# Layer norms of a transformer kernel: root on ScalarE and reciprocal on VectorE, or a power on GpSimd

## The chip, the cores and the metric

The kernel runs on one core of one Trainium2 chip. The metric is the device time of one execution in microseconds (us), and several executions are summed up by their median. TensorE (PE in the rows) multiplies matrices, VectorE (DVE) and ScalarE (ACT) do elementwise work and reductions, GpSimd (POOL) does elementwise work in on-chip memory only, and SyncE (SP) issues the transfers. Each engine works through its own queue in order, and they wait for each other on semaphores.

## What is computed

2048 tokens of width 128 pass through six residual blocks, each behind a layer norm. Stage A is a coupled feed-forward net, B a causal attention, C the feed-forward net again, D a mixture of eight experts, E an attention with low-rank updates, and F the mixture again. Block B also ends in a norm of its own with scale and offset, called M here. Only the norm matters for the change:

```python
def _layernorm(x, axis=-1, eps=1e-05):
    m = jnp.mean(x, axis=axis, keepdims=True)
    v = jnp.var(x, axis=axis, keepdims=True)
    return (x - m) / jnp.sqrt(v + eps)

x = L0_attn_target
x = x + 0.5 * _L0_ffn_ref(_layernorm(x, axis=-1), ...)   # A
x = x + _L0_attn_ref(_layernorm(x, axis=-1), ...)        # B; norm M inside
x = x + 0.5 * _L0_ffn_ref(_layernorm(x, axis=-1), ...)   # C
x = x + 0.5 * _L1_ffn_ref(_layernorm(x, axis=-1), ...)   # D
x = x + _L1_attn_ref(_layernorm(x, axis=-1), ...)        # E
x = x + 0.5 * _L1_ffn_ref(_layernorm(x, axis=-1), ...)   # F
```

## The kernel before, in words

The activations lie feature by feature on the 128 partitions, with the 2048 tokens along the free axis, cut into four chunks of 512 (`NC = 4`, `CW = 512`). The order of work on every engine is written out by hand, and nothing is scheduled by a planner around the norms. The norms are called `LN_A` to `LN_F` and `LN_M`.

A norm of one chunk is a relay over three engines, each step a method of class `Norm`:

1. `pe_centre` (line 274): TensorE multiplies by a centring matrix. The result is x minus its mean, in a PSUM bank.
2. `act_square` (line 325) squares it on ScalarE, and `dve_centre` (line 297) copies it to `m_cen` on VectorE.
3. `pe_var` (line 282): four small products sum the squares over the features. The variances of the 512 tokens lie in a 128x128 block.
4. `act_root` (line 336): ScalarE takes the root of variance plus epsilon, into `m_std`, 128x128 per chunk.
5. `dve_invert` (line 307): VectorE takes the reciprocal of `m_std` in place.
6. `pe_spread` (line 289): four products spread the reciprocals back over all partitions.
7. `dve_norm` (line 311) or `dve_affine` multiplies and gives the normed chunk.

TensorE, ScalarE and VectorE take their steps of the four chunks interleaved, so that one chunk's step on an engine stands in the queue between steps of other chunks. `LN_M` and `LN_C` go in pairs of chunks: LN_M 0 and 1, LN_M 2 and 3, LN_C 0 and 1, LN_C 2 and 3, and each pair's `pe_var` stands behind the `pe_spread` of the pair before it on TensorE. `LN_D` runs into stage D, and `LN_E` and `LN_F` are interleaved with the end of the stage before and the start of their own; chunk 0 of LN_E and chunk 3 of LN_F lie inside an expert stage.

ScalarE's functions come out of loaded tables. `warm(function)` (line 2000) is a tiny activation that is there to bring in a table early, as `warm(ACT.Sqrt)` ahead of the norms; where there is none, the load stands in front of the activation that needs it (lines 336, 829, 801). GpSimd has other work near the norms: `pool_low` (line 1263) makes the third bf16 part of queries and keys from each chunk of an attention, and the expert stage's `pool` (lines 790, 792) splits each normed chunk.

Of the kernel before, what the change touches and what calls it, by code (L numbers as in the profile page):

```python
# [9 lines left out]
fp32 = mybir.dt.float32  # L10
# [71 lines left out]
class Constants:  # L82
# [7 lines left out]
    def __init__(self, nc, n, dram, k):  # L90
# [12 lines left out]
        k["eps"] = n.sb("eps", [P, 1], fp32)  # L103
        k["fold"] = n.sb("fold", [P, 2], fp32)
# [82 lines left out]
    def dve(self, dve):  # L187
        nc, k = self.nc, self.k
        nc.vector.memset(k["eps"][:, :], EPS)
        for b, sign in enumerate((1.0, -1.0, -1.0, 1.0)):  # L190
            nc.vector.memset(k["sign"][32 * b:32 * b + 32, :], sign)
# [69 lines left out]
class Norm:  # L261


    def __init__(self, nc, n, ps, k, centres=True):
        self.nc, self.ps, self.k = nc, ps, k
# [20 lines left out]
    def pe_spread(self, pe, i, c, bank):  # L286
        pe.wait_ge(self.inverted, NC * i + c + 1)
        for u in range(TPC):
# [16 lines left out]
    def dve_invert(self, dve, i, c):  # L305
        dve.wait_ge(self.std_ready, NC * i + c + 1)
        self.nc.vector.reciprocal(self.std[:, c, :], self.std[:, c, :]).then_inc(self.inverted, 1)  # L307

# [25 lines left out]
    def act_root(self, act, i, c, bank):  # L334
        act.wait_ge(self.var_ready, NC * i + c + 1)
        self.nc.scalar.activation(self.std[:, c, :], self.ps[:, bank, 0:TW], ACT.Sqrt, bias=self.k["eps"][:, 0:1])\
# [288 lines left out]
class Experts:  # L625
# [157 lines left out]
    def pool(self, pool):  # L783
        k = self.k
        for c in range(NC):
            pool.wait_ge(self.norm.out, NC * self.ln + c + 1)
# [51 lines left out]
    def dve(self, dve):  # L838
# [99 lines left out]
        else:  # L938
# [11 lines left out]
            norm.dve_invert(dve, self.ln, last)  # L950
            add(1)
            norm.dve_norm(dve, self.ln, last, self.xn, self.SPARE)
        for i in range(self.begin, len(steps)):
# [16 lines left out]
            if ln is not None:  # L970
                if i == 11:
                    norm.dve_centre(dve, ln, 0, self.SPARE)
                elif i == 14:
                    norm.dve_invert(dve, ln, 0)
# [736 lines left out]
def macaron(nc, dram, out):  # L1711
    with ExitStack() as stack:
# [50 lines left out]
        with nc.Block() as block:  # L1763
# [14 lines left out]
            def _(pool):  # L1778
                constants.pool(pool)
                for c in range(NC):  # L1780
                    att_b.pool_low(pool, c)
                att_b.pool_loop(pool)
                constants.pool_experts(pool)
                moe_d.pool(pool)
                for c in range(NC):
                    att_e.pool_low(pool, c)
                att_e.pool_loop(pool)
                moe_f.pool(pool)
# [112 lines left out]
            def _(dve):  # L1901
# [15 lines left out]
                def ffn_end(ffn, ln, bank):  # L1917
# [5 lines left out]
                    norm.dve_invert(dve, ln, 0)  # L1923
                    norm.dve_centre(dve, ln, 3, bank + 3)
                    norm.dve_invert(dve, ln, 1)
                    norm.dve_norm(dve, ln, 0, xn, bank)
                    norm.dve_invert(dve, ln, 2)
                    norm.dve_norm(dve, ln, 1, xn, bank + 1)
                    norm.dve_invert(dve, ln, 3)
# [15 lines left out]
                def b_end(phase, c):  # L1945
# [7 lines left out]
                    elif phase == 2:  # L1953
                        norm_m.dve_invert(dve, LN_M, c)
                    elif phase == 3:
                        norm_m.dve_affine(dve, LN_M, c, xn, x, NC + c, x_done)
                    elif phase == 5:
                        norm.dve_invert(dve, LN_C, c)
# [18 lines left out]
                norm.dve_invert(dve, LN_E, 1)  # L1977
# [3 lines left out]
                norm.dve_invert(dve, LN_E, 2)  # L1981
                norm.dve_invert(dve, LN_E, 3)
# [5 lines left out]
                norm.dve_invert(dve, LN_F, 0)  # L1988
                norm.dve_invert(dve, LN_F, 1)
# [137 lines left out]
```

## Time and profile before

| | us |
|---|---|
| three runs | 1308.64, 1314.72, 1324.19 (median 1314.72) |
| the profiled execution | 1311.64 |
| its span from first to last instruction | 1309.8 |
| PE busy | 1246.0 (95%) |
| DVE busy | 1147.0 (88%) |
| ACT busy | 1061.3 (81%) |
| POOL busy | 183.0 (14%) |

The profiled execution's own time is 1.8 us more than its span. Busy shares are averages over stages with different limits: both attentions together fill the stretches from about 75 to 456 us and from about 616 to 1233 us, and the norms in question lie in the short stretches between.

### The profile page before, as it was taken

How to read it: one execution, taken by the hardware profiler on the slowest of the kernel's cores; microseconds unless marked ns; L12 is line 12 of the kernel's file. 1: busy time of each engine (PE TensorE's matmuls, PEld its weight loads, DVE VectorE, ACT ScalarE, POOL GpSimd, SP SyncE). 2: the span in 40 equal slices, each digit the busy share in tenths (PEclk: the TensorE clock that was granted, in tenths of full speed). 3: DMA queues.
4: the chain of work that ended last, by engine and by line, in shares of the span. 5: the costliest groups of instructions: out<-in, count | busy, mean ns of one | idle time of the engine just before them, and what ended most of it. 6: DMA issues, size and time to landing. Idle time of an engine off the chain costs nothing. (4 is left out here: it accounts for less than half of the span.)

```text
span 1309.8 us, 30395 instructions
## 1 busy us (share of the span) xinstructions
PE 1246.0 (95%) x11960; PEld 454.0 (35%) x12022; DVE 1147.0 (88%) x1528; ACT 1061.3 (81%) x2064; POOL 183.0 (14%) x463
## 2 busy tenths in 40 slices
PE   7889999999999988999899999999999999999998
PEld 3253332332333352555223323333233332333454
DVE  6878989999999377766999999999999999998375
ACT  4657887898999946435599999999999999999641
POOL 9234221211111100112000000000000000000100
PEclk9999999999999999899999999999999999999999
DMA  5251310500000012002321000000000000000000
GB/s 135 57 141 45 50 19 20 63 5 13 4 3 3 5 42 65 1 1 73 97 61 43 3 4 13 4 4 3 13 4 4 4 3 13 4 4 2 13 9 25
DMA packets 38525, 35.11 MB, mean 27 GB/s; under 512 B 16080, under 2 KB 31920, under 8 KB 38384
## 3 DMA queue, kind: packets, MB, share of 16 engines
q1 hardware_dynamic: 38384, 33.17, 10.9%
q8 instruction: 95, 1.56, 0.5%
q14 instruction: 46, 0.38, 0.1%
HBM read 17.03 MB, written 9.70 MB: 20 GB/s over the span
## 5 line engine op out<-in xcount | busy, mean ns | idle before, releaser
L1583 DVE TENSOR_REDUCE m_blockmax<-ps 128x2 f32<-128x1024 f32 (+1 forms) x768 | 873.2, 1205 | 22.7 <-PE ps L1394 14.2
L1547 ACT ACTIVATE m_prob<-ps 128x512 f32<-128x512 f32 (+3 forms) x1664 | 849.0, 576 | 40.4 <-PE ps L1432 31.4
L1394 PE MATMUL ps<-m_k_all,m_q_all 64*128 64x512 bf16 (+2 forms) x1732 | 321.3, 376 | 16.4 <-DVE m_blockmax L1583 12.0
L1432 PE MATMUL ps<-m_q_max,m_k_all 64*128 64x512 bf16 (+3 forms) x1664 | 332.8, 366 | 0.5
L1455 PE MATMUL ps<-m_prob,m_v_op 128*9 128x256 f32 x4096 | 317.0, 381 | 0.1
L1394 PEld LDWEIGHTS ps<-m_k_all,m_q_all 64*128 64x128 bf16 x1732 | 82.0, 93 | 332.4 <-DVE m_blockmax L1583 225.1
L1451 PE MATMUL ps<-m_prob,m_v_op 128*9 128x256 f32 (+3 forms) x2560 | 177.9, 350 | 0.8 <-ACT m_prob L1547 0.3
L1432 PEld LDWEIGHTS ps<-m_q_max,m_k_all 64*128 64x128 bf16 x1664 | 147.1, 94 | 89.2 <-ACT m_prob L1547 36.6
L1606 POOL CAST m_maxparts<-m_negmax 128x8 bf16<-128x8 f32 x64 | 14.0, 218 | 703.4 <-DVE m_negmax L1562 698.3
L1455 PEld LDWEIGHTS ps<-m_prob,m_v_op 128*9 128x9 f32 x4096 | 60.9, 88 | 129.8 <-issue 117.7
L829 ACT ACTIVATE m_prob<-ps 128x512 f32<-128x512 f32 x40 | 23.8, 596 | 64.3 <-PE ps L692 54.3
L1625 POOL TENSOR_SCALAR_AFFINE_SELECT m_prob<-m_prob 128x256 f32<-128x256 f32 x128 | 51.3, 406 | 126.7 <-ACT m_prob L1547 125.2
L1451 PEld LDWEIGHTS ps<-m_prob,m_v_op 128*9 128x9 f32 x2560 | 38.3, 88 | 78.9 <-issue 53.7
L1538 ACT ACTIVATE m_q_max<-ps 128x512 bf16<-128x512 f32 x64 | 38.2, 597 | 27.8 <-PE ps L1416 27.3
L916 DVE TENSOR_TENSOR m_prob<-m_prob,ps 128x512 f32<-128x512 f32 x32 | 22.0, 687 | 25.4 <-PE ps L720 24.4
L1577 DVE CUSTOM_DVE_ANT_0 m_sq<-ps,m_mask_q 128x256 bf16<-128x256 f32 (+1 forms) x128 | 39.8, 350 | 1.8 <-PE ps L1394 1.5
L274 PE MATMUL ps<-m_x,m_centre_of 128*128 128x512 f32 x42 | 25.5, 705 | 12.8 <-DVE m_x L565 6.8
L289 PE MATMUL ps<-m_std,m_row_of 128*128 128x128 f32 x224 | 32.0, 295 | 4.9 <-DVE m_std L307 4.9
L690 PE MATMUL ps<-m_x_parts,m_e_parts 128*128 128x512 f32 x64 | 35.3, 551 | 1.3 <-DVE m_prob L911 1.2
L702 PE MATMUL ps<-m_prob,m_e_down 128*128 128x512 f32 x64 | 35.1, 635 | 0.0
L1416 PE MATMUL ps<-m_identb,m_maxparts 128*128 128x128 bf16 x256 | 24.7, 219 | 9.9 <-ACT m_prob L1547 8.4
L289 PEld LDWEIGHTS ps<-m_std,m_row_of 128*128 128x128 f32 x224 | 29.6, 206 | 12.6 <-issue 6.6
(232 smaller groups left out, 966.7 us busy)
## 6 DMA issues: line engine op xcount, KB each, us to landing
m_part<-m_xn SPq DMA_DIRECT2D x48, 128.0 KB, 2.4
ba_parts<-m_part SPq DMA_DIRECT2D x8, 384.0 KB, 5.3
ea_parts<-m_part SPq DMA_DIRECT2D x8, 384.0 KB, 2.6
m_k_all<-ea_parts SPq DMA_DIRECT2D x84, 32.0 KB
m_q_all<-ea_parts SPq DMA_DIRECT2D x84, 32.0 KB
m_k_all<-ba_parts SPq DMA_DIRECT2D x36, 64.0 KB
m_q_all<-ba_parts SPq DMA_DIRECT2D x36, 64.0 KB
m_x<-in_x SPq DMA_DIRECT2D x4, 256.0 KB, 3.9
```

The lines of the kernel that those rows point to most:

```text
L289: mm = pe.matmul(tile(self.ps[:, bank, :], u), self.k["row_of"][:, u, :], self.std[:, c, :], start=True, stop=True, skip_group_check=True)
L690: pe.matmul(ps[:, bank, :], w_hi, x_hi, start=True, stop=False)
L702: pe.matmul(ps[:, self.DOWN, :], wd, k["hid"][:, i % 2, :], start=(shared or g == 0), stop=(shared or g == GROUPS - 2)).then_inc(self.down ...
L1394: mm = pe.matmul(ps[:, MX + 2 * (u % 2) + j, 0:width], q_all[head, pair, q0:q0 + TW], k_all[head, pair, CW * kc:CW * kc + width], start=Tr ...
L1432: pe.matmul(ps[:, e % ST, q0:CW], k_all[head, pair, TW * i:TW * i + TW], q_max[m % 2][head, q0:CW], start=True, stop=True).then_inc(self.s ...
L1451: mm = pe.matmul(ps[VC * g:VC * g + VW, SUM, HALF * first:HALF_CW], weights, own, start=(i == 0), stop=True, skip_group_check=True)
L1455: mm = pe.matmul(ps[VC * g:VC * g + VW, SUM, 0:HALF_CW], weights, own, start=(i == 0), stop=True, skip_group_check=True)
L1538: nc.scalar.activation(q_max[m % 2][:, :], ps[:, e % ST, :], ACT.Copy).then_inc(self.st_used, 1)
L1547: nc.scalar.activation(prob[:, (2 * t + j) % NP, q0:CW], ps[:, e % ST, q0:CW], ACT.Exp, scale=SCALE)\
L1577: reduce = nc.vector.tensor_tensor_reduce(k["hidden"][:, u % 2, j, 0:width], ps[:, MX + 2 * (u % 2) + j, 0:width], k["mask_q"][:, 2 * TW - ...
L1583: nc.vector.tensor_reduce(blockmax[:, m % plan.AHEAD, qt, :, kc], ps[:, MX + 2 * (u % 2):MX + 2 * (u % 2) + 2, 0:width], AX.X, ALU.max)\
L1625: pool.affine_select(out=own, in_=own, compare_op=ALU.is_ge, fill=0.0, base=0, pattern=[[0, 2], [1, TW]], channel_multiplier=-1).then_inc( ...
```

## The change

For all norms but LN_A, ScalarE only adds epsilon (`Identity` with a bias) and VectorE's reciprocal is gone. In their place GpSimd raises the 128x128 block to the power -1/2 with a two-input instruction, whose second input is a block `k["power"]` filled with -0.5. Nothing else is computed differently. `pe_spread` waits for `centred` too, which the reciprocal's place in VectorE's queue used to imply. The `warm(ACT.Sqrt)` calls behind LN_A are dropped. The 24 powers are placed in GpSimd's queue by hand.

```diff
     def pe_spread(self, pe, i, c, bank):
         pe.wait_ge(self.inverted, NC * i + c + 1)
+        if self.centres and i > 0:
+            pe.wait_ge(self.centred, NC * i + c + 1)
...
+    def pool_power(self, pool, i, c):
+        pool.wait_ge(self.std_ready, NC * i + c + 1)
+        pool.tensor_tensor(self.std[:, c, :], self.std[:, c, :], self.k["power"][:, :], ALU.pow).then_inc(self.inverted, 1)
...
     def act_root(self, act, i, c, bank):
         act.wait_ge(self.var_ready, NC * i + c + 1)
-        self.nc.scalar.activation(self.std[:, c, :], self.ps[:, bank, 0:TW], ACT.Sqrt, bias=self.k["eps"][:, 0:1])\
+        function = ACT.Sqrt if self.centres and i == 0 else ACT.Identity
+        self.nc.scalar.activation(self.std[:, c, :], self.ps[:, bank, 0:TW], function, bias=self.k["eps"][:, 0:1])\
             .then_inc(self.std_ready, 1)
...
     def pool(self, pool):
         k = self.k
         for c in range(NC):
+            if c == 2 and self.before is not None:
+                self.norm.pool_power(pool, self.ln, NC - 1)
...
                 constants.pool(pool)
+                pool.wait_ge(constants.filled, 1)
+                for c in range(NC):
+                    norm.pool_power(pool, LN_B, c)
                 for c in range(NC):
                     att_b.pool_low(pool, c)
                 att_b.pool_loop(pool)
                 constants.pool_experts(pool)
+                for t in range(8):
+                    for c in range(NC):
+                        if t - c // 2 == 2:
+                            norm_m.pool_power(pool, LN_M, c)
+                        elif t - c // 2 == 5:
+                            norm.pool_power(pool, LN_C, c)
+                for c in range(NC):
+                    norm.pool_power(pool, LN_D, c)
                 moe_d.pool(pool)
-                for c in range(NC):
+                norm.pool_power(pool, LN_E, 0)
+                norm.pool_power(pool, LN_E, 1)
+                att_e.pool_low(pool, 0)
+                norm.pool_power(pool, LN_E, 2)
+                norm.pool_power(pool, LN_E, 3)
+                for c in range(1, NC):
                     att_e.pool_low(pool, c)
                 att_e.pool_loop(pool)
+                for c in range(NC - 1):
+                    norm.pool_power(pool, LN_F, c)
                 moe_f.pool(pool)
...
                 def ffn_end(ln, bank, then):
-                    warm(ACT.Sqrt)
                     for c in range(3):
...
-                warm(ACT.Sqrt)
                 for c in (0, 1, 2):
                     norm.act_root(act, LN_F, c, 5 + c)
```

VectorE's queue at LN_B before, from the copy of chunk 0 on (`m_cen<-ps` is the copy, `m_xn<-m_cen,ps` the normed chunk):

```order
L297 COPY m_cen<-ps 128x512 x2
L307 RECIPROCAL m_std<-m_std 128x128
L297 COPY m_cen<-ps 128x512
L307 RECIPROCAL m_std<-m_std 128x128
L311 TENSOR_TENSOR m_xn<-m_cen,ps 128x512
L307 RECIPROCAL m_std<-m_std 128x128
L311 TENSOR_TENSOR m_xn<-m_cen,ps 128x512
L307 RECIPROCAL m_std<-m_std 128x128
```

The same place with the change:

```order
L571 TENSOR_TENSOR m_xn<-m_prob 128x512
L574 SCALAR_TENSOR_TENSOR m_x<-m_xn,m_x 128x512
L301 COPY m_cen<-ps 128x512 x3
L319 TENSOR_TENSOR m_xn<-m_cen,ps 128x512 x2
L1266 TENSOR_TENSOR m_sq<-ps,m_part 128x512
```

The four reciprocals between the copies and the products are gone.

GpSimd's queue from the split of the expert weights, through LN_M, LN_C, LN_D and stage D, to LN_E; before, the splits of stage D are followed by the first `pool_low` of stage E:

```order
L157 TENSOR_TENSOR m_e_parts<-m_part,m_e_parts 128x512
L790 CAST m_x_parts<-m_xn 128x512
L792 TENSOR_TENSOR m_x_parts<-m_xn,m_x_parts 128x512
...
L1263 TENSOR_TENSOR m_part<-m_sq,m_part 128x512
L1263 TENSOR_TENSOR m_part<-m_cen,m_part 128x512
```

With the change (L315 is the power, L1271 is `pool_low`):

```order
L158 TENSOR_TENSOR m_e_parts<-m_part,m_e_parts 128x512
L315 TENSOR_TENSOR m_std<-m_std,m_power 128x128 x12
L801 CAST m_x_parts<-m_xn 128x512
L803 TENSOR_TENSOR m_x_parts<-m_xn,m_x_parts 128x512
...
L315 TENSOR_TENSOR m_std<-m_std,m_power 128x128 x2
L1271 TENSOR_TENSOR m_part<-m_sq,m_part 128x512
L1271 TENSOR_TENSOR m_part<-m_cen,m_part 128x512
L315 TENSOR_TENSOR m_std<-m_std,m_power 128x128 x2
L1271 TENSOR_TENSOR m_part<-m_sq,m_part 128x512
L1271 TENSOR_TENSOR m_part<-m_cen,m_part 128x512
```

Twelve powers (LN_M, LN_C, LN_D) stand ahead of stage D's splits, two (LN_E 0 and 1) behind them, and two (LN_E 2 and 3) between `pool_low` of chunk 0 and that of chunk 1.

ScalarE's queue at LN_F before, behind the last sums of stage E:

```order
L1521 ACTIVATE m_cen<-ps 128x256
L2000 ACT_TABLE_LOAD
L2000 ACTIVATE m_warm<-m_eps 128x1
L336 ACTIVATE m_std<-ps,m_eps 128x128 x3
L829 ACT_TABLE_LOAD
L829 ACTIVATE m_prob<-ps 128x512
```

With the change:

```order
L1529 ACTIVATE m_cen<-ps 128x256
L345 ACTIVATE m_std<-ps,m_eps 128x128 x3
L840 ACT_TABLE_LOAD
L840 ACTIVATE m_prob<-ps 128x512
```

A table load and the warming activation are gone from between the sums and the three chunks of LN_F. Over the whole program the ScalarE queue has 24 table loads before and 15 with the change.

## Rows read from the trace of the kernel before

**Rows 1.** The page, part 1: busy time of each engine, its share, xinstructions

```profile
PE 1246.0 (95%) x11960; PEld 454.0 (35%) x12022; DVE 1147.0 (88%) x1528; ACT 1061.3 (81%) x2064; POOL 183.0 (14%) x463
```

**Rows 2.** One line's instructions: reciprocal (L307); spread's wait behind it, after LN_A

```profile
L307 DVE RECIPROCAL m_std<-m_std x28: 894/944/953, 12.1 to 1255.3; 128x128 f32<-128x128 f32 x28
...
  DVE m_std L307: 8.7, 8
```

**Rows 3.** Groups of ScalarE: busy us, mean ns, idle before

```profile
L2000 ACT ACT_TABLE_LOAD x9 | 11.5, 1283 | 1.0 <-PEq L2119 0.8
...
L336 ACT ACT_TABLE_LOAD x2 | 2.6, 1283 | 0.0
```

**Rows 4.** Groups of GpSimd by shape: busy us, mean ns, idle before

```profile
L1625 POOL TENSOR_SCALAR_AFFINE_SELECT m_prob<-m_prob 128x256 f32<-128x256 f32 x128 | 51.3, 406 | 126.7 <-ACT m_prob L1547 125.2 <-PE ps L1432 0.9 <-PE ps L1416 0.4
...
L1608 POOL TENSOR_TENSOR m_maxrest<-m_negmax,m_maxparts 128x8 f32<-128x8 f32 x64 | 13.1, 205 | 5.3
...
L1263 POOL TENSOR_TENSOR m_part<-m_sq,m_part 128x512 bf16<-128x512 f32 x8 | 9.3, 1158 | 75.3 <-ACT m_part L1238 75.3
```

**Rows 5.** Timeline of LN_B: start us, duration us, engine, line, operation [idle before, releaser]

```profile
61.05 0.36 ACT L336 ACTIVATE m_std<-ps,m_eps 128x128 f32<-128x128 f32 x1
...
63.23 0.94 DVE L307 RECIPROCAL m_std<-m_std 128x128 f32<-128x128 f32 x1
...
63.83 0.36 ACT L336 ACTIVATE m_std<-ps,m_eps 128x128 f32<-128x128 f32 x1
...
64.23 1.16 PE L289 MATMUL ps<-m_std,m_row_of 128*128 128x128 f32 x8 [0.58 <-DVE m_std L307]
...
65.67 1.16 PE L289 MATMUL ps<-m_std,m_row_of 128*128 128x128 f32 x8
...
71.55 1.05 PE L289 MATMUL ps<-m_std,m_row_of 128*128 128x128 f32 x8
```

**Rows 6.** Timeline of LN_M and LN_C, ScalarE's roots and TensorE's spreads, by pairs

```profile
466.40 0.62 ACT L336 ACTIVATE m_std<-ps,m_eps 128x128 f32<-128x128 f32 x2 [0.46 <-PE ps L282]
...
470.00 1.95 PE L289 MATMUL ps<-m_std,m_row_of 128*128 128x128 f32 x16
...
477.47 0.62 ACT L336 ACTIVATE m_std<-ps,m_eps 128x128 f32<-128x128 f32 x2 [1.09 <-PE ps L282]
...
480.19 2.02 PE L289 MATMUL ps<-m_std,m_row_of 128*128 128x128 f32 x16
...
482.62 0.62 ACT L336 ACTIVATE m_std<-ps,m_eps 128x128 f32<-128x128 f32 x2 [1.15 <-PE ps L282]
...
484.53 1.95 PE L289 MATMUL ps<-m_std,m_row_of 128*128 128x128 f32 x16
```

**Rows 7.** Timeline of LN_D, chunk 1: root and spread

```profile
530.92 0.37 ACT L336 ACTIVATE m_std<-ps,m_eps 128x128 f32<-128x128 f32 x1
...
533.38 1.83 PE L289 MATMUL ps<-m_std,m_row_of 128*128 128x128 f32 x8
```

**Rows 8.** Timeline of LN_E, chunk 2: root, GpSimd's work there, spread

```profile
607.08 0.36 ACT L336 ACTIVATE m_std<-ps,m_eps 128x128 f32<-128x128 f32 x1
...
607.86 1.15 POOL L1263 TENSOR_TENSOR m_part<-m_cen,m_part 128x512 bf16<-128x512 f32 x1
...
608.59 1.16 PE L289 MATMUL ps<-m_std,m_row_of 128*128 128x128 f32 x8 [0.39 <-DVE m_std L307]
```

**Rows 9.** Timeline of LN_F, chunks 0 to 2, then the load behind chunk 3

```profile
1234.20 1.28 ACT L2000 ACT_TABLE_LOAD   x1
...
1235.61 0.86 ACT L336 ACTIVATE m_std<-ps,m_eps 128x128 f32<-128x128 f32 x3
...
1236.99 2.93 PE L289 MATMUL ps<-m_std,m_row_of 128*128 128x128 f32 x16 [2.60 <-DVE m_std L307]
...
1256.22 1.28 ACT L829 ACT_TABLE_LOAD   x1
```

**Rows 10.** One stretch: length, PE, PEld, DVE, ACT, POOL busy, granted clock, DMA

```profile
1236.00:1240.00 4.00, 3.01 (x17) 3.01 (x18) 3.34 (x5) 1.75 (x3) 0.92 (x2) 0.75 0.28 76
```

More of the change, by code:

```diff
@@ L103, in __init__ @@
         k["eps"] = n.sb("eps", [P, 1], fp32)
+        k["power"] = n.sb("power", [P, TW], fp32)
         k["fold"] = n.sb("fold", [P, 2], fp32)
@@ L189, in dve @@
         nc.vector.memset(k["eps"][:, :], EPS)
+        nc.vector.memset(k["power"][:, :], -0.5)
         for b, sign in enumerate((1.0, -1.0, -1.0, 1.0)):
@@ L264, in __init__ @@
     def __init__(self, nc, n, ps, k, centres=True):
-        self.nc, self.ps, self.k = nc, ps, k
+        self.nc, self.ps, self.k, self.centres = nc, ps, k, centres
         self.std = k["std"]
@@ L949, in dve @@
             add(0)
-            norm.dve_invert(dve, self.ln, last)
             add(1)
@@ L972, in dve @@
                     norm.dve_centre(dve, ln, 0, self.SPARE)
-                elif i == 14:
-                    norm.dve_invert(dve, ln, 0)
                 elif i == 16:
@@ L1922, in ffn_end @@
                     norm.dve_centre(dve, ln, 2, bank + 2)
-                    norm.dve_invert(dve, ln, 0)
                     norm.dve_centre(dve, ln, 3, bank + 3)
-                    norm.dve_invert(dve, ln, 1)
                     norm.dve_norm(dve, ln, 0, xn, bank)
-                    norm.dve_invert(dve, ln, 2)
                     norm.dve_norm(dve, ln, 1, xn, bank + 1)
-                    norm.dve_invert(dve, ln, 3)
                 ffn_a.dve_bias(dve)
@@ L1952, in b_end @@
                         att_b.dve_add(dve, c, NC + c)
-                    elif phase == 2:
-                        norm_m.dve_invert(dve, LN_M, c)
                     elif phase == 3:
                         norm_m.dve_affine(dve, LN_M, c, xn, x, NC + c, x_done)
-                    elif phase == 5:
-                        norm.dve_invert(dve, LN_C, c)
                     elif phase == 6 and c < 2:
@@ L1975, in _ @@
                 moe_d.dve(dve)
-                norm.dve_invert(dve, LN_E, 1)
                 att_e.dve_rest(dve, 0)
@@ L1980, in _ @@
                 norm.dve_norm(dve, LN_E, 1, xn, Experts.TURN)
-                norm.dve_invert(dve, LN_E, 2)
-                norm.dve_invert(dve, LN_E, 3)
                 norm.dve_norm(dve, LN_E, 2, xn, Experts.SPARE)
@@ L1986, in _ @@
                 att_e.dve_loop(dve)
-                norm.dve_invert(dve, LN_F, 0)
-                norm.dve_invert(dve, LN_F, 1)
                 norm.dve_norm(dve, LN_F, 0, xn, 5)
-                norm.dve_invert(dve, LN_F, 2)
                 norm.dve_norm(dve, LN_F, 1, xn, 6)
@@ L2057, in _ @@
                 moe_d.act(act)
-                warm(ACT.Sqrt)
                 norm.act_root(act, LN_E, 1, Experts.TURN)
@@ L2072, in _ @@
                 att_e.act_loop(act)
-                warm(ACT.Sqrt)
                 for c in (0, 1, 2):
```

## The prediction

> **What bounds the kernel now.** I read the page's busy line first [rows 1]: TensorE 95% and VectorE 88% of a 1309.8 us span, GpSimd 14%. That says GpSimd has room, but not when. The stretches that the change touches are short, and there each chunk's norm is a relay in which every engine waits for another, so the answer is in the timelines of the norms. I read for each norm when ScalarE's root ends and when TensorE's spread begins. The difference is the room that any inversion has before it costs something. The line view of the spread gives the total prize: after LN_A, TensorE sat idle behind reciprocals for 8.7 us in 8 waits [rows 2]. An inversion in no time at all could win little more than that.
>
> **What is removed.** 24 reciprocals of 0.94 us on VectorE [rows 2], 22.6 us busy. TensorE waits for few of them, and where VectorE is dense (LN_B, LN_C) the spread stands right behind other TensorE work, so I count their removal only where the spread comes earlier. Nine table loads of 1.28 us on ScalarE [rows 3], 11.5 us busy: five warmed ones, two roots inside the expert stages and the two loads back behind those. Most lie where ScalarE waits for TensorE anyway. Two are exposed: the one ahead of LN_F at 1234.20, behind which the roots start only at 1235.61, and the one at 1256.22 ahead of an expert activation, of which I take 0.9 of 1.28 us as on the path [rows 9]. A load ends just before the next activation begins there and takes nothing beside its 1.28 us. The Trainium skill ("ScalarE: Activation LUTs", section "What ACT_TABLE_LOAD costs") adds a drain of about 1.38 us to each switch. By that, an exposed load would be worth 2.66 us and LN_F would give 1.4 us more; the trace shows no such gap.
>
> **What is added: the power, of length p.** No row shows a power. The nearest rows from below are GpSimd's two-input subtractions: 205 ns for 8 columns, 1158 ns for 512 [rows 4], hence 1.9 ns a column and 0.43 us for 128 columns, if the power were as cheap as a subtraction. The one-input select, 406 ns for 256 columns [rows 4], gives no more. From above: I assume that a general power takes a logarithm, a product and an exponential in software, 10 to 20 elementary steps. If each cost a full pass at 1.9 ns a column, 128 columns would take 2.4 to 4.9 us and 0.2 us to start. If the steps overlap they cost less, and if special cases are handled one by one, more. I take **p = 3 us**, nearer to the passes than to the one subtraction, because reading two operands is not what a power is made of, and I keep 0.43 and 5.5 us as ends. The Trainium skill speaks against elementwise work on GpSimd at all ("GPSIMD Engine Reference", "Elementwise — side-by-side cycle accounting"): a two-input operation takes about 2.6 cycles an element, twice VectorE's time. That is near the slope in the rows, and if it held for the power too, p would be near the low end and the sum below would be a small gain.
>
> **The sum at p = 3.** A power starts 0.1 us behind the end of ScalarE's instruction, and the spread 0.1 us behind the power; the reciprocal's end at 64.17 and the spread at 64.23 show such a handover [rows 5]. All powers of a norm stand in one queue, so the second is done two lengths after the first began.
>
> - LN_B [rows 5]: first root ends at 61.41, so the second power ends at 61.51 + 6 = 67.51 and its spread starts at 67.6 in place of 65.67: **+1.9**. Later chunks have room at this p: the fourth power ends at 73.5, its spread was at 71.55 and is pushed by 1.9 anyway.
> - LN_M and LN_C [rows 6], four pairs in series, since a pair's variances stand on TensorE behind the spreads of the pair before. In a pair, the second power ends 0.36 + 0.1 + 6 after the roots begin, and the second spread was half-way in its row. First pair: 466.40 + 6.56 = 472.96 against 470.98, +2.0. Second and third pair (the same pattern; the third is shown): 477.47 + 6.56 = 484.03 against 481.20, +2.8 each. Fourth: 482.62 + 6.56 = 489.18 against 485.50, +3.7. Together **+11.3**. Behind it, stage C's global sum needs all four chunks, so nothing gives this back.
> - LN_D [rows 7]: 530.92 + 0.37 + 3.2 = 534.49 against 533.38: **+1.1**. Stage D's splits of x move behind the powers too, but their products come after the shared ones; I take nothing.
> - LN_E, chunk 2 [rows 8]: here the queue matters. The power stands behind `pool_low` of chunk 0, which ends at 609.01, though the root is there at 607.44. The spread comes at 609.01 + 3.1 = 612.1 against 608.59: **+3.5**. Queued behind that wait on TensorE are chunk 1's queries and keys and all the building for attention E; the attention waits for them. Chunks 0 and 1 have several us of room.
> - LN_F [rows 9]: the roots start at 1234.20. The second power ends at 1234.56 + 6.1 = 1240.66, its spread starts at 1240.76 against half of the row at 1236.99, 1238.45: **+2.3**. Chunk 3's power stands in a free GpSimd.
> - The exposed load in stage F: **-0.9**.
>
> 1.9 + 11.3 + 1.1 + 3.5 + 2.3 - 0.9 = 19.2. The profiled execution took 1311.64 us, 1.8 more than its span, which I keep: 1330.9. The runs' median is 3.1 above the profiled one and the lowest 3.0 below. I say **1332**. Beside this, where TensorE waited 2.6 us ahead of LN_F's spreads, the granted clock of 1236 to 1240 was 0.75, a mean of both levels (2.4 and 1.2 GHz) [rows 10], and the spreads of two chunks took 2.93 us where 1.95 us is usual [rows 6, 9]. Longer waits in the other norms could add an estimated 1 us each, not in the sum.
>
> **Rivals.**
>
> *The power is cheap* (p under 2). At p = 2 the same terms read +0.7, +3.3, +0.1, +2.5, +0.3, -0.9, together +6. At p = 1: -0.3, -0.3, 0, +1.5, -1.7, -0.9, together -2. At the low end, 0.43, about -4. So the time lies between 1308 and 1318, and the turning point is p of about 1.2. This is the other side of my forecast: one mechanism, a power that hardly exceeds the reciprocal's 0.94 us, with LN_F and the table loads as the gain. For it speak GpSimd's low share and the subtraction's row; against it that LN_E pays the queue behind `pool_low` at any p.
>
> *The power is dear* (p over 4.5). Then the fourth chunk of LN_B is late as well, 61.41 + 4p against 71.55. At p = 5: 10.1 + 27.3 + 3.1 + 5.5 + 6.3 - 0.9 = 51, 1363 us. Each further us costs about 18 (4 + 8 + 1 + 2 + 2, and the chunks that now join). At p = 8 it is over 1415.
>
> *A gain over 1%.* It would need more than 13 us. The 8.7 us of waits plus the 2.2 us of exposed loads do not reach that, even with the clock at LN_F held up; the drain of the skill's page would add 1.4 at each exposed load. I leave 5% for what I do not see, a load that delays more than the rows tell.
>
> **How the numbers follow.** About 1% (13 us) is what a measurement of this kernel can tell from no change, as its three runs are 15 us apart. The forecast, p from 2 to 4.5, gets 0.42, of which 0.32 is above 13 us (from p = 2.5 on) and 0.10 below; cheap 0.33; dear 0.20; a gain 0.05. Slower 0.52, same 0.43, faster 0.05. The range goes from 1306 (the low end's 1308, less run scatter) to 1375 (p = 5.5: 51 us at 5 plus half of 18, and a little for the clock); that leaves the gain and the dearer part of the dear case outside, under 0.2. The likeliest case alone spans 1318 to 1355.
>
> **What would show it.** GpSimd's row for the power gives p at once: 128x128, 24 times. Right would be: the waits of the spread (line 293 of the changed kernel) name GpSimd in place of VectorE, with some 20 us after LN_A; the second to fourth pair from LN_M on come 8 us or more apart where they are 5 apart now; LN_E's power starts right behind `pool_low`; 15 table loads. The prediction is wrong if p is below 2 or above 4.5, or if the attentions absorb a late start, which I have excluded for B and E because they are dense from their first product on.

## The result: a third slower, because one power takes 20.8 us

| | before | after |
|---|---|---|
| median of the runs, us | 1313.88 (4 runs) | 1773.49 (4 runs) |
| lowest and highest | 1308.64, 1324.19 | 1769.37, 1773.85 |
| the profiled execution | 1311.64 | 1773.85 |
| its span | 1309.8 | 1771.9 |
| mean granted clock of the span | 0.991 | 0.860 |

The changed kernel takes 1.349 times as long, with an interval from 1.344 to 1.354. The prediction's 1332 misses this by 441 us and the upper end of its range, 1375, by 398; only the sign was right. Two executions that took over 1.5% more than the fastest of their kernel are in no median and no ratio below: one of 2724 us of the kernel with six products, and one of 1349.79 us of the narrow kernel with root and reciprocal.

The page of the changed kernel shows where to look. Its first part is the busy time of each engine [rows 1]; its second shows the span in 40 slices, GpSimd's row (POOL) and the granted clock of TensorE in tenths.

```profile
PE 1295.5 (73%) x11960; PEld 482.2 (27%) x12022; DVE 1129.5 (64%) x1505; ACT 1050.1 (59%) x2050; POOL 682.9 (39%) x487
...
POOL 8596421111118999279359500000000000004950
PEclk9768999999996555865886799999999999998569
```

GpSimd is 500 us busier. VectorE and ScalarE have about the work that they had. TensorE has the same number of products and is busy for 50 us more, at a lower mean clock. All three stand idle for most of the 462 us that the span has grown. GpSimd's high digits and the low clock stand in the same slices: around LN_B (slices 2 to 4), from LN_M to LN_E (13 to 23), and at LN_F (37 to 39). The group rows of the page, with busy us, mean ns, and the idle time before them by releaser, name the cause:

```profile
L315 POOL TENSOR_TENSOR m_std<-m_std,m_power 128x128 f32<-128x128 f32 x24 | 499.3, 20822 | 147.8 <-ACT m_std L345 147.8
...
L293 PE MATMUL ps<-m_std,m_row_of 128*128 128x128 f32 x224 | 53.7, 417 | 417.9 <-POOL m_std L315 342.2
```

One power of a 128x128 block takes 20,822 ns on average, and the 24 lie between 20.76 and 21.27 us. The reciprocal that it replaces took 944 [rows 2], and GpSimd's subtraction with four times the columns 1158 [rows 4]. The spread waits 342 us for it in waits that the profile puts down to the power, and of the rest 74 us stand as "issue" behind the same powers at LN_C.

The timeline shows the powers and the last spread of each stage (start us, duration us, operation, idle time before it and its releaser). GpSimd first:

```profile
64.64 83.02 POOL L315 TENSOR_TENSOR m_std<-m_std,m_power 128x128 f32<-128x128 f32 x4 [23.09 <-ACT m_std L345]
...
543.98 41.52 POOL L315 TENSOR_TENSOR m_std<-m_std,m_power 128x128 f32<-128x128 f32 x2 [6.66 <-ACT m_std L345]
...
588.72 41.85 POOL L315 TENSOR_TENSOR m_std<-m_std,m_power 128x128 f32<-128x128 f32 x2 [3.22 <-ACT m_std L345]
...
928.33 20.78 POOL L315 TENSOR_TENSOR m_std<-m_std,m_power 128x128 f32<-128x128 f32 x1 [15.29 <-ACT m_std L345]
949.08 1.16 POOL L1271 TENSOR_TENSOR m_part<-m_sq,m_part 128x512 bf16<-128x512 f32 x1
950.19 1.16 POOL L1271 TENSOR_TENSOR m_part<-m_cen,m_part 128x512 bf16<-128x512 f32 x1
951.30 41.53 POOL L315 TENSOR_TENSOR m_std<-m_std,m_power 128x128 f32<-128x128 f32 x2
```

Then TensorE, the last chunk's spread of LN_B, LN_C, LN_D, LN_E and LN_F:

```profile
147.71 2.07 PE L293 MATMUL ps<-m_std,m_row_of 128*128 128x128 f32 x8 [16.25 <-POOL m_std L315]
...
720.49 2.04 PE L293 MATMUL ps<-m_std,m_row_of 128*128 128x128 f32 x8 [18.70 <-issue]
...
847.98 2.08 PE L293 MATMUL ps<-m_std,m_row_of 128*128 128x128 f32 x8 [15.25 <-POOL m_std L315]
...
992.88 2.07 PE L293 MATMUL ps<-m_std,m_row_of 128*128 128x128 f32 x8 [15.59 <-POOL m_std L315]
...
1715.62 2.08 PE L293 MATMUL ps<-m_std,m_row_of 128*128 128x128 f32 x8 [18.51 <-POOL m_std L315]
```

In the kernel before, the last spread of LN_B began at 71.55 [rows 5] and that of LN_C at half of the last row of [rows 6], 485.50. The other three are rows of the same timeline of the kernel before:

```profile
541.71 1.05 PE L289 MATMUL ps<-m_std,m_row_of 128*128 128x128 f32 x8
...
611.31 1.05 PE L289 MATMUL ps<-m_std,m_row_of 128*128 128x128 f32 x8
...
1257.42 1.05 PE L289 MATMUL ps<-m_std,m_row_of 128*128 128x128 f32 x8
```

A stage's loss is how much further apart these marks lie than those of the stage before:

| up to the last spread of | later by, us | of which new | powers in it |
|---|---|---|---|
| LN_B | 76.2 | 76.2 | 4 |
| LN_C | 235.0 | 158.8 | 8 |
| LN_D | 306.3 | 71.3 | 4 |
| LN_E | 381.6 | 75.3 | 4 |
| LN_F | 458.2 | 76.6 | 4 |
| the end | 462.1 | 3.9 | 0 |

Four powers in a row take 83.0 to 83.5 us, and each group of four costs 71 to 79. The loss of 462 us is nearly as long as the 499 us of power. Some 2.3 us of LN_B's 76.2 lie ahead of the norm: its first centring began at 57.35, before at 55.04. In the kernels below with the same code ahead of LN_B it began between 54.48 and 60.45, so that part is scatter between executions and no cost of the change. It also makes any difference of two spans uncertain by a few us.

The spreads show the second cost. Each takes 2.04 to 2.08 us, where 1.16 and 1.05 us were usual [rows 5]. TensorE had been idle for 12.6 to 21.0 us before each, and comes back at its lower clock of 1.2 GHz. Over the stretch of LN_M and LN_C (length, PE, PEld, DVE, ACT and POOL busy, granted clock, DMA) the clock was 0.55, and TensorE was busy for a fifth of the time:

```profile
538.00:725.00 187.00, 37.00 (x167) 23.30 (x166) 15.62 (x23) 13.16 (x27) 166.72 (x8) 0.55 0.03 7
```

### The profile page after: what moved, and what is told of

Same layout as the page of the kernel before. It is cut to its first block and busy times, and to the rows that moved or that the text cites. A ratio compares the mean times of both kernels' runs of the same rounds, so it can differ in the third digit from the quotient of the medians.

```text
span 1771.9 us, 30399 instructions
## 1 busy us (share of the span) xinstructions
PE 1295.5 (73%) x11960; PEld 482.2 (27%) x12022; DVE 1129.5 (64%) x1505; ACT 1050.1 (59%) x2050; POOL 682.9 (39%) x487
## 5 line engine op out<-in xcount | busy, mean ns | idle before, releaser
L1591 DVE TENSOR_REDUCE m_blockmax<-ps 128x2 f32<-128x1024 f32 (+1 forms) x768 | 872.8, 1201 | 22.1 <-PE ps L1402 15.8
L315 POOL TENSOR_TENSOR m_std<-m_std,m_power 128x128 f32<-128x128 f32 x24 | 499.3, 20822 | 147.8 <-ACT m_std L345 147.8
L293 PE MATMUL ps<-m_std,m_row_of 128*128 128x128 f32 x224 | 53.7, 417 | 417.9 <-POOL m_std L315 342.2
L319 DVE TENSOR_TENSOR m_xn<-m_cen,ps 128x512 f32<-128x512 f32 x24 | 16.3, 684 | 368.8 <-PE ps L293 368.8
L293 PEld LDWEIGHTS ps<-m_std,m_row_of 128*128 128x128 f32 x224 | 46.5, 308 | 432.0 <-POOL m_std L315 353.5
L345 ACT ACTIVATE m_std<-ps,m_eps 128x128 f32<-128x128 f32 x28 | 9.7, 369 | 225.5 <-PE ps L284 225.2
L1459 PEld LDWEIGHTS ps<-m_prob,m_v_op 128*9 128x9 f32 x2560 | 38.3, 88 | 79.1 <-issue 53.5
L927 DVE TENSOR_TENSOR m_prob<-m_prob,ps 128x512 f32<-128x512 f32 x32 | 22.0, 688 | 47.1 <-PE ps L729 45.8
```

Of the source, the lines that this page charges most:

```text
L293: mm = pe.matmul(tile(self.ps[:, bank, :], u), self.k["row_of"][:, u, :], self.std[:, c, :], start=True, stop=True, skip_group_check=True)
L315: pool.tensor_tensor(self.std[:, c, :], self.std[:, c, :], self.k["power"][:, :], ALU.pow).then_inc(self.inverted, 1)
L1459: mm = pe.matmul(ps[VC * g:VC * g + VW, SUM, HALF * first:HALF_CW], weights, own, start=(i == 0), stop=True, skip_group_check=True)
L1591: nc.vector.tensor_reduce(blockmax[:, m % plan.AHEAD, qt, :, kc], ps[:, MX + 2 * (u % 2):MX + 2 * (u % 2) + 2, 0:width], AX.X, ALU.max)\
```

## The experiments

Two theories had to be told apart first. By one, the 462 us are the power's own length, in series. By the other, the structure is at fault too: the moved queue, the missing warm-ups, the extra wait in the spread. For the sum there was a third question, whether its terms hold at the power length for which they were made.

### The chain without the power

```diff
-        nc.vector.memset(k["power"][:, :], -0.5)
+        nc.vector.memset(k["power"][:, :], 0.01)
...
-        pool.tensor_tensor(self.std[:, c, :], self.std[:, c, :], self.k["power"][:, :], ALU.pow).then_inc(self.inverted, 1)
+        pool.tensor_tensor(self.std[:, c, :], self.std[:, c, :], self.k["power"][:, :], ALU.mult).then_inc(self.inverted, 1)
```

> The changed kernel with a product in place of the power (and 0.01 in place of -0.5 in the second operand), so that the norms' scales are not the reference's. Theory 1, the whole loss is the length of the power: a product of 128x128 takes about 0.43 us on GpSimd, and the prediction's sum for that length gives 1308 us (-4 against the kernel before), the queue behind pool_low in LN_E costing 0.9 us and LN_F winning some. Rival, a part of the loss comes from what else the change brings (the added wait for the copy, the powers' places in GpSimd's queue, a slower clock that stays): the time stays above 1330 us.

Median 1312.28 us over 10 runs, against 1315.5 for the kernel before on the same chip: ratio 0.999, from 0.996 to 1.002. The groups of GpSimd give the product's length:

```profile
L315 POOL TENSOR_TENSOR m_std<-m_std,m_power 128x128 f32<-128x128 f32 x24 | 11.1, 476 | 169.3 <-ACT m_std L345 169.3
```

So the whole loss comes from the power's length, with what a longer wait brings along. The 24 reciprocals, 9 table loads and the new queue together are worth nothing that can be measured. This is also the ceiling of the idea: with an inversion of half a microsecond on GpSimd it would gain at most 0.4%. The timeline at LN_E chunk 2 shows the queue behind `pool_low`, which the prediction priced at any length of power:

```profile
605.61 1.16 POOL L1271 TENSOR_TENSOR m_part<-m_sq,m_part 128x512 bf16<-128x512 f32 x1 [5.61 <-ACT m_part L1246]
...
605.95 0.36 ACT L345 ACTIVATE m_std<-ps,m_eps 128x128 f32<-128x128 f32 x1
...
606.73 1.15 POOL L1271 TENSOR_TENSOR m_part<-m_cen,m_part 128x512 bf16<-128x512 f32 x1
...
...
607.84 0.87 POOL L315 TENSOR_TENSOR m_std<-m_std,m_power 128x128 f32<-128x128 f32 x2
...
608.35 1.16 PE L293 MATMUL ps<-m_std,m_row_of 128*128 128x128 f32 x8 [1.28 <-POOL m_std L315]
```

ScalarE is done with chunk 2 at 606.31, and GpSimd begins its product only at 607.84, as `pool_low` ends: 1.5 us of queue. The products of chunks 2 and 3 are merged in one row. The spread comes 3.69 us behind that of chunk 1, at 604.66. Before it was 2.80 behind (608.59 against 605.79). So this queue costs 0.9 us net, as the product is shorter than the reciprocal. At LN_F the spreads came after 0.64 us of waiting in place of 2.60 [rows 9].

### Half of the columns

The power works on 64 of the 128 columns, and a product by 0.01 stands ahead of it for the others.

```diff
+        pool.tensor_tensor(self.std[:, c, 64:], self.std[:, c, 64:], self.k["power"][:, 64:], ALU.mult)
+        pool.tensor_tensor(self.std[:, c, 0:64], self.std[:, c, 0:64], self.k["power"][:, 0:64], ALU.pow).then_inc(self.inverted, 1)
```

> The changed kernel with the power on 64 of the 128 columns and a product on the other 64 (scales of half of the tokens not the reference's). If the power's time goes by columns (20.77 us for 128, 162 ns a column), an instruction takes 10.4 us and, with 24 of them in series, the time is near 1773 - 24 x 10.1 = 1530 us. If it is a fixed cost of starting the operation, the instruction stays near 20 us and the time near 1773 or above.

Median 1539.65 us, ratio 1.172 (1.168 to 1.176). By shape:

```profile
L317 POOL TENSOR_TENSOR m_std<-m_std,m_power 128x64 f32<-128x64 f32 x24 | 253.2, 10550 | 0.0
...
L316 POOL TENSOR_TENSOR m_std<-m_std,m_power 128x64 f32<-128x64 f32 x24 | 8.3, 345 | 153.5 <-ACT m_std L347 153.5
```

64 columns take 10.55 us and 128 take 20.82, hence 160 ns a column. The length goes with the columns, and there is no large fixed part. Product and power together last 10.9 us, and the span is 227.4 us over that of before. Of this, 5.4 us lie ahead of LN_B, whose first centring began at 60.45 in this execution.

### Another exponent

The exponent is -1. The kernel ran once.

```diff
-        nc.vector.memset(k["power"][:, :], -0.5)
+        nc.vector.memset(k["power"][:, :], -1.0)
```

> The changed kernel with the exponent -1 in place of -1/2, so that the scale is 1 over the variance and not the reference's. If the power is one general routine, its row stays at 20.8 us and the time near 1773. If the length depends on the exponent or on the values, the row changes, for instance towards 10 us or less for a whole exponent.

1773.93 us, and 24 powers of 20,837 ns. The price is that of the operation, not of this exponent. Only these two exponents were tried.

### The change at LN_M and LN_C alone

The kernel before, with the eight powers of LN_M and LN_C, and roots and reciprocals everywhere else. Against the changed kernel:

```diff
+    def powered(self, i):
+        return not self.centres or i == 2
...
-        function = ACT.Sqrt if self.centres and i == 0 else ACT.Identity
+        function = ACT.Identity if self.powered(i) else ACT.Sqrt
```

> The kernel before with the change made for LN_M and LN_C alone (8 powers of 24; one table load less in front of them), computing the same. The prediction's term for these norms is 8p less 12.4: at p = 20.8 it reads 154 us, a few more for TensorE at the half clock between the waits: 1470 us, one third of the whole loss. If the losses at the several norms were not in series with each other, so that a late start of one is absorbed in a stage behind it, the time would be clearly less, under 1440.

Median 1470.32 us, ratio 1.121 (1.115 to 1.126), 157 us over the 1313.05 of its comparison. The changed kernel lost 158.8 there, so the stages' losses add up and do not hide each other. Two of the pairs on GpSimd:

```profile
514.04 41.84 POOL L316 TENSOR_TENSOR m_std<-m_std,m_power 128x128 f32<-128x128 f32 x2 [3.23 <-ACT m_std L346]
559.11 41.84 POOL L316 TENSOR_TENSOR m_std<-m_std,m_power 128x128 f32<-128x128 f32 x2 [3.23 <-ACT m_std L346]
```

They begin 45.07 us apart: 41.84 of power and 3.23 of relay over TensorE and ScalarE. With nothing beside it, this is a series.

### The length for which the prediction was made

In place of the power stand six products by 0.7, each waiting for the one before it. This gives a chain of 3.1 us and tests the sum at its own p.

```diff
-        pool.tensor_tensor(self.std[:, c, :], self.std[:, c, :], self.k["power"][:, :], ALU.pow).then_inc(self.inverted, 1)
+        for n in range(PASSES):
+            if n > 0:
+                pool.wait_ge(self.inverted, PASSES * (NC * i + c) + n)
+            pool.tensor_tensor(self.std[:, c, :], self.std[:, c, :], self.k["power"][:, :], ALU.mult).then_inc(self.inverted, 1)
```

> The changed kernel with six products in a row, each waiting for the one before, in place of the power, so that the norms' scales are not the reference's. A single product took 0.48 us in the run before, so the chain should take 3.0 us or a little more with the handovers. If the prediction's sum was right and only its p was wrong, the time is 19 us above that of the kernel before, between 13 and 26. If the sum was wrong too, for instance because longer waits in the norms halve the clock, it is over 30 us above; if the norms hide 3 us, it is within 6 us of it.

Median 1357.34 us over three runs, ratio 1.029 (1.022 to 1.037). The profiled one is 45.8 us over the span of before, the medians are 44 apart, and the ratio's interval gives 29 to 48. The prediction's terms at 3.1 us make about 21. So the sum was too small at its own length too. By the same marks as above, the last spread of each stage:

```profile
79.00 1.05 PE L294 MATMUL ps<-m_std,m_row_of 128*128 128x128 f32 x8
...
512.11 1.59 PE L294 MATMUL ps<-m_std,m_row_of 128*128 128x128 f32 x8 [1.94 <-issue]
...
572.70 1.05 PE L294 MATMUL ps<-m_std,m_row_of 128*128 128x128 f32 x8
...
649.22 1.05 PE L294 MATMUL ps<-m_std,m_row_of 128*128 128x128 f32 x8
...
1301.48 1.16 PE L294 MATMUL ps<-m_std,m_row_of 128*128 128x128 f32 x8 [0.84 <-POOL m_std L319]
```

| | measured, us | the prediction's term at 3.1 |
|---|---|---|
| LN_B | 7.5, of it 2.3 ahead of the first chain | 2.1 |
| LN_M and LN_C | 19.2 | 12.1 |
| LN_D | 4.4 | 1.2 |
| LN_E | 6.9 | 3.6 |
| LN_F, with the load | 6.2 | 1.6 |
| rest | 1.7 | 0 |

At LN_B the rows tell where the excess of 5.4 us over the term comes from. TensorE's projections behind the second spread (line 1218, before line 1206) are:

```profile
67.12 1.98 PE L1206 MATMUL ps<-m_xn,m_wqkv 128*128 128x512 f32 x4
...
73.48 3.07 PE L1218 MATMUL ps<-m_xn,m_wqkv 128*128 128x512 f32 x4
```

From the second spread to the third it is 5.5 us (70.89 to 76.39) where it was 3.3 (65.67 to 68.94): the spread, a variance and the projections between them run at half clock, wholly or in part, which is 2.2 us. The other 3.1 us lie ahead of the first chain, which begins at 64.65 in place of 61.51. Of them 2.3 are the late start, and 0.8 go with a half clock that two kernels without a long wait, the product kernel and the one of the last experiment, also show there (a centring of 1.74 and 1.69 us for 1.12). The third and the fourth spread stand behind the projections and wait for no chain, so at 3.1 us not all powers of a norm are in series.

What is missing at LN_M and LN_C stands in GpSimd's timeline, pair by pair:

```profile
475.79 6.75 POOL L319 TENSOR_TENSOR m_std<-m_std,m_power 128x128 f32<-128x128 f32 x12 [6.71 <-ACT m_std L349]
485.76 7.07 POOL L319 TENSOR_TENSOR m_std<-m_std,m_power 128x128 f32<-128x128 f32 x12 [3.23 <-ACT m_std L349]
496.06 6.51 POOL L319 TENSOR_TENSOR m_std<-m_std,m_power 128x128 f32<-128x128 f32 x12 [3.23 <-ACT m_std L349]
```

The pairs come 10 us apart. Two chains last 6.5 to 7.1 us in these three, not 6.2. From the second spread (482.59) to the next chain it is 3.2 us. Before, it was 1.9: from 481.20 to 483.08, where the power would have begun, 0.1 behind the end of the first of the two roots at 482.62 [rows 6]. The second spread of the pair comes behind a wait and at half clock, and takes 2.07 us:

```profile
482.59 2.07 PE L294 MATMUL ps<-m_std,m_row_of 128*128 128x128 f32 x8 [2.47 <-POOL m_std L319]
```

Over the whole span TensorE was busy for 1272.9 us here and for 1246.0 before, with 11960 products recorded in both: the same work took 26.9 us longer, 8.9 of them in the spreads, 5.9 in the centrings and 2.9 in the variances. This does not split the loss exactly, as not every product is on the chain that ends last. But 45.8 less 26.9 is 19, near the sum's 21, so the clock can be most of what the sum lacked.

### The same with TensorE kept busy

In front of 15 of the spreads (the expectation says 19; the edit reaches 15, and the trace has 150 weight loads for the fillers) TensorE multiplies ten times into the bank that the spread is about to overwrite. Against the kernel with six products:

```diff
+            pe.wait_ge(self.std_ready, NC * i + c + 1)
...
+            for _ in range(FILL):
+                pe.matmul(self.ps[:, bank, :], self.k["identb"][:, :],
+                          self.k["select"][:, 0, 0:2, :, :].rearrange("p a b r -> p (a b r)"), start=True, stop=True)
         pe.wait_ge(self.inverted, PASSES * (NC * i + c + 1))
```

> The kernel with six products in place of the power, and in front of 19 of the spreads, where TensorE waits for GpSimd, ten products of 128x512 into the spread's own bank (their result is overwritten; some 2.2 us at the full clock, inside a wait of about 3 us). The scales are still not the reference's. The six products alone cost 38 to 46 us where the sum allows 21. If the missing part is TensorE's clock, which fell to half behind the waits (spreads of 2.08 us in place of 1.16), this kernel should be some 12 to 20 us faster than that one, 1335 to 1345, with spreads of 1.16 us. If the missing part is something else (waits that the sum did not count), the time stays at 1350 or more.

Median 1349.07 us, 8 less than without the fillers, and ratio 1.025 (1.019 to 1.031) to before. The spreads are back at 1.05 to 1.16 us:

```profile
484.62 2.32 PE L297 MATMUL ps<-m_select,m_identb 128*128 128x512 bf16 x10
...
486.77 1.05 PE L303 MATMUL ps<-m_std,m_row_of 128*128 128x128 f32 x8
```

The two intervals overlap, so the 8 us are no firm number; less was gained than expected, and 37 us of loss stay. This does not show that they are no matter of the clock, since the fillers cost time themselves. At LN_B they delay the spreads (70.36 and 73.87, where they were 67.81 and 70.89). In the first pair of LN_M the second spread comes 9.3 us behind the begin of the chains (486.77 and 477.50), without fillers 6.8 (482.59 and 475.79). Up to the last spread of LN_D, by which 12 of the 15 groups of fillers have run, nothing is gained (572.94 against 572.70); the gain stands from LN_E on. So what the half clock costs in all at this length is not measured by this pair of kernels. For the relay it is: from the second spread (486.77) to the next chain it is 1.9 us again, where 3.2 had been without fillers and 1.9 before:

```profile
488.70 6.54 POOL L328 TENSOR_TENSOR m_std<-m_std,m_power 128x128 f32<-128x128 f32 x12 [4.98 <-ACT m_std L358]
```

The changed kernel itself with 80 fillers in front of each of the 24 spreads:

```diff
+        if FILL and (not self.centres or i > 0):
+            pe.wait_ge(self.std_ready, NC * i + c + 1)
```

> The changed kernel, computing the same, with 80 such products (17 us at the full clock) in front of each of the 24 spreads behind a power of 20.8 us. The loss of 460 us is put down to 24 powers in series (my terms at p = 20.8 give 424) and to the half clock behind each wait (the rest, some 30 us). With the clock held up the time should fall by 20 to 35 us, to 1738 to 1753. If the clock is not part of it, it stays at 1773; if the products are too long for the wait, it rises.

Median 1759.96 us (1750.21 to 1763.49), 14 less than the changed kernel; the profiled one was 24 less, 2.7 of it ahead of LN_B. In the stretch of LN_M and LN_C the clock is 0.97 with TensorE busy for 172 of 187 us, against 0.55:

```profile
538.00:725.00 187.00, 172.38 (x812) 79.31 (x820) 20.61 (x34) 18.92 (x38) 166.06 (x8) 0.97 0.04 9
```

So holding the clock up gives back 14 to 24 of the 462 us, and the expected time of 1738 to 1753 was missed by the median. The waits themselves remain.

### A narrow block

If a power costs 160 ns a column, 4 columns cost under 1 us. The variances of a chunk are laid out as 128 tokens by 4 columns, by changing which operand is the weight:

```diff
-            mm = pe.matmul(self.ps[32 * u:32 * u + 32, bank, 0:TW], self.k["var_of"][:, :], tile(self.k["sq"], TPC * c + u),
+            mm = pe.matmul(self.ps[:, bank, u:u + 1], tile(self.k["sq"], TPC * c + u), self.k["var_of"][:, 0:1],
...
-            mm = pe.matmul(tile(self.ps[:, bank, :], u), self.k["row_of"][:, u, :], self.std[:, c, :],
+            mm = pe.matmul(tile(self.ps[:, bank, :], u), self.std[:, c, u:u + 1].to_broadcast([P, P]), self.k["ident"][:, :],
...
-        pool.tensor_tensor(self.std[:, c, :], self.std[:, c, :], self.k["power"][:, :], ALU.pow).then_inc(self.inverted, 1)
+        pool.tensor_tensor(self.std[:, c, 0:TPC], self.std[:, c, 0:TPC], self.k["power"][:, 0:TPC], ALU.pow).then_inc(self.inverted, 1)
```

> The changed kernel computing the same, with the variances laid out as 128 tokens by 4 columns (the squares as stationary operand against one column of 1/128), the power on 128x4, and the spread as a product of the column, broadcast, with the identity. By columns, a power takes 0.2 + 4 x 0.162 = 0.85 us, and the time is near that of the kernel before: 1305 to 1312 us, with the 9 table loads gone and one queue wait in LN_E. If a power has a large fixed cost, its row shows more than 3 us and the time is over 1330.

The same layout with the root and the reciprocal of the kernel before:

```diff
-        self.nc.vector.reciprocal(self.std[:, c, :], self.std[:, c, :]).then_inc(self.inverted, 1)
+        self.nc.vector.reciprocal(self.std[:, c, 0:TPC], self.std[:, c, 0:TPC]).then_inc(self.inverted, 1)
```

> The kernel before (root and reciprocal) in the same narrow layout of 128x4, computing the same. The reciprocal should fall from 0.94 us to about 0.2, the root from 0.37 to 0.2; the stationary loads of the variance get wider (128 columns in place of 32). The prediction's terms give 2 to 4 us of gain in LN_B, LN_C and LN_F: 1308 to 1312 us. If the wider loads and the extra steps of TensorE cost more than that, the time is at or over that of the kernel before. Against the narrow power it tells which of the two ways is better when the power is short.

Medians 1336.64 us with the power (ratio 1.017, 1.014 to 1.020) and 1332.41 over three runs with root and reciprocal (1.012, 1.006 to 1.018). Both are slower than before, and both expectations were missed. The narrow power is short, as it should be. As the kernel with root and reciprocal is slower too, the layout is at fault, and the rows show what it costs TensorE. The kernel with the power, by shape:

```profile
L315 POOL TENSOR_TENSOR m_std<-m_std,m_power 128x4 f32<-128x4 f32 x24 | 24.6, 1030 | 174.5 <-ACT m_std L345 174.5
...
L293 PE MATMUL ps<-m_ident,m_std 128*128 128x128 f32 x224 | 36.4, 321 | 1.1 <-POOL m_std L315 1.1
...
L284 PE MATMUL ps<-m_var_of,m_sq 128*128 128x1 f32 x224 | 32.0, 270 | 0.6 <-DVE m_cen L301 0.6
```

and the variance products of the kernel before, in the same view:

```profile
L282 PE MATMUL ps<-m_sq,m_var_of 128*32 128x128 f32 x224 | 10.6, 290 | 0.6 <-DVE m_cen L297 0.6
```

With the squares as weight, the products are busy for 32.0 us in place of 10.6, though each gives one column (the mean of one overlaps its neighbours and says less than the busy time). The spread adds 4.4 (36.4 against 32.0). TensorE's busy time is 1285.8 us. The trace of the kernel before lacks 62 of its products, so the 1246.0 there is too low for a comparison; the product kernel, with the same layout as before and all 12022 recorded, has 1255.8. By that, TensorE is 30.0 us busier, and 25.8 of them are these two. The span is 22.8 longer than before. At equal layout, a power of 1.03 us cannot be told from root and reciprocal (263 and 172 ns in the second kernel): the intervals overlap.

### The kernel before with its clock kept up

The fillers in the kernel before, at its three gaps (ahead of stage B's last sums, in LN_D's centring, ahead of LN_F's spreads):

```diff
                         if c == NC - 1:
                             pe.wait_ge(att_b.sums_ready, att_b.plan.count)
+                            keep_clock(12, c)
...
                 for c in (0, 1, 2):
                     norm.pe_var(pe, LN_F, c, 5 + c)
+                keep_clock(12, 4)
```

> The kernel before, computing the same, with such products in the three gaps behind which its granted clock falls: 12 while stage B's last sums come in (462 to 465 us), 3, 3 and 4 in front of LN_D's centring, 12 in front of LN_F's first spread. At the half clock its rows show the projections with 3.68 us for 1.99, LN_D's centring and spreads 2.08 for 1.1, LN_F's two spreads 2.93 for 1.95. Holding the clock up should be worth 4 to 7 us: 1306 to 1310 us, a ratio of 0.995 to 0.997. If the waits there are for others anyway, it changes nothing.

Median 1309.8 us over 12 runs against 1312.36 over 16, ratio 0.998 (0.995 to 1.000). That is 0.2% by the medians and 0.5% at most, and the interval touches no change. LN_F's spreads take 2.05 us in place of 2.93 [rows 9]:

```profile
1233.19 2.54 PE L1795 MATMUL ps<-m_select,m_identb 128*128 128x512 bf16 x11 [0.16 <-issue]
1235.64 2.05 PE L289 MATMUL ps<-m_std,m_row_of 128*128 128x128 f32 x16
```

## Why the prediction was wrong

**The step that failed** is the price of the power: "I take p = 3 us", with 0.43 and 5.5 us as ends. It measured 20.8 us. The upper end came from 10 to 20 elementary steps at the 1.9 ns a column of GpSimd's subtraction [rows 4], thus at most 38 ns a column. The power takes 160 ns a column, 84 times a subtraction's slope. No row of the kernel before showed a power, a root or any other function on GpSimd, and the bound rested on an assumed algorithm. The sentence kept a door open, "if special cases are handled one by one, more", and gave it no number. This alone puts the time out of the range. Of its cases, *the power is dear* is the one that came, and it had 0.20. Why a column costs 160 ns, whether by number of steps or by their length, is not known from here.

**The cycle count cited from the Trainium skill** ("GPSIMD Engine Reference", "Elementwise — side-by-side cycle accounting") was set beside the subtraction's 1.9 ns a column, and the product agrees with that: 345 ns for 64 and 476 for 128 columns, 2.0 a column. It does not hold for the power. The drain of about 1.38 us that the Trainium skill ("ScalarE: Activation LUTs", "What ACT_TABLE_LOAD costs") adds to a table load was not seen: ahead of LN_F the load ends at 1235.48 and the roots begin at 1235.61 [rows 9]. The product kernel, with nine loads fewer, gains nothing that can be measured.

**The second step, the growth with p**, was mis-sized. "Each further us costs about 18" counted 17 powers in series and one for chunks that join. The spans give 45.8 us of loss at 3.1, 227.4 at 10.9 and 462.1 at 20.8: 23.3 per us, then 23.7 (22.9, then 24.0, without what lies ahead of LN_B's first centring). So beyond 3.1 us nearly all 24 powers are in series, though at 3.1 us itself some spreads still wait for no chain. LN_E's chunks 0 and 1, for which I saw "several us of room", and the chunks of LN_D and LN_F that the terms leave out have none once the chunk before them in GpSimd's queue is late. This step matters beside the first: with p = 20.8 the rule of 18 gives 51 + 15.8 x 18 = 335 us, 127 less than was lost. (The 424 us in the expectation of the kernel with 80 fillers do not follow from that rule.)

**The sum at its own p** gave 21 where 29 to 48 were measured. One part is the clock, which the text named ("an estimated 1 us each, not in the sum") and should have added. TensorE's same work took 26.9 us longer, which bounds it from above only roughly; the fillers gave back 8 and cost time themselves. Another part is the relay behind each pair, 3.2 us where 1.9 had been, and that is the clock as well, since with fillers it is 1.9 again. At LN_B the excess is the late start and the clock. LN_D, LN_E and LN_F each cost 3 to 5 us more than their terms, and how much of that is clock is open.

**The total prize** was read too high. The 8.7 us in 8 waits [rows 2] are those of TensorE's products and of its weight loads together, and these stand idle side by side for the same reciprocal. Taken alone, after LN_A:

```profile
  DVE m_std L307: 3.6, 3
```

for the products, and 5.1 us in 5 waits for the weight loads. An inversion in no time could thus win about 4 to 5 us at the waits of the spreads, not 9. The forecast of a loss does not use the number, only the argument against a gain over 1%, which it would have made stronger.

**What held.** LN_M and LN_C by the prediction's own formula, with 20.8 in place of 3, give 37.5 + 38.3 + 38.3 + 39.2 = 153 us; 157 and 158.8 were measured. LN_B's fourth power at 61.51 + 4p, less 71.55, gives 73; measured were 76.2 with the 2.3 us from ahead of it. The spread's waits name GpSimd, the table loads are 15, LN_E's third power starts right behind `pool_low` (951.30 behind 950.19 + 1.16), and its queue cost 0.9 us with a cheap operation, as its term gives. The cheap rival's value at p of 0.43, about 4 us of gain, lies inside the interval of the product kernel; so does no gain at all, and the spans differ by 0.5 us. A gain over 1% was rightly held unlikely: the ceiling is 0.4%.

## What to carry to other kernels

Before a function is moved to an engine on which the profile shows none, its length must be measured at the shape in question, because the range of an unmeasured price is not set by the elementwise rows beside it. Put a cheap operation in its place first: here that showed in one run that the best case was worth nothing, whatever the power cost. In a relay where one engine inverts for all chunks in a queue, count every operation as in series once it is longer than the time between two chunks, and add TensorE's half clock behind each wait.

## What the runs showed of the hardware

- GpSimd's two-input power took 1.03, 10.55 and 20.82 us for 4, 64 and 128 columns of 128 partitions in float32. That is about 0.4 us and 0.16 us a column, and 20.84 us for 128 columns with the exponent -1. The product took 0.48 us for 128 columns and 0.35 for 64.
- Spreads of one chunk behind waits of 12.6 to 21.0 us took 2.04 to 2.08 us; in the kernel with six products and ten fillers ahead of 15 of them, all took 1.05 to 1.16. In the kernel before, this effect is worth at most 0.5%.
- Products of one column with a 128x128 float32 weight kept TensorE busy for 143 ns each (32.0 us over 224), those of 128 columns with a 128x32 weight for 47 ns (10.6 over 224). Their weight loads were busy for 33.0 us against 5.1. The narrow result saved TensorE nothing; the layout cost it more.
